# The condition product by samples in two row halves, its second half inside the first group

## Chip, core and metric

One core of one Trainium2 chip runs the kernel. The metric is the device time of one execution, in microseconds (us). The kernel before was timed three times: 1285.14, 1284.44 and 1283.88 us, median 1284.44 us.

## What is computed

```python
W = weights[condition]                     # 32 samples, each picks one of 16 matrices of 64 x 64
c = einsum('bct,bcd->bdt', x, W)           # x: (32, 64, 1024)
h = gelu(einsum('bsd,df->bsf', c, inter_w) + inter_b)   # 1024 -> 4096
out = x + einsum('bsf,fd->bsd', h, output_w) + output_b # 4096 -> 1024
```

All is float32. The 32 samples of 64 rows are 2048 rows of 1024 features for the two large products.

## The kernel before, in words

**The passes.** The rows are worked in two passes `h` of 1024 rows: 8 pairs of samples (`TILES`), two samples of 64 rows to a pair. Each of the two large products is done by a Strassen scheme: 7 products (`PRODUCTS`) in place of 8. Each product takes three matmuls (high by high, high by low, low by high): its operands are split into a float32r part and the rest: ScalarE (ACT) writes the high part with a copy, VectorE (DVE) subtracts it to give the low part. Stage one (`first`, lines 468 to 503) has 8 groups `g` of 512 hidden features with 14 steps `c` each (7 products, two halves `p`); a step is 12 matmuls of 128x512, so a stage of a pass is 1344. Stage two (`second`, lines 505 to 519) has as many.

**The condition product** (`cond`, lines 454 to 466) turns x into the transposed activations y. One matmul takes a pair of samples: a 128x128 block of x is the stationary operand, a row of `wdiag` the moving one, in which the two samples' 64x64 matrices stand on the diagonal. GpSimd (POOL) fills `wdiag` (lines 406 to 420): zeros first, then 32 copies in a loop of 16, each chosen by an index read from `itok_sb`. `cond` runs four times ahead of the first large product: for each pass `h` and each half `n` of its pairs, over 4 pairs and 8 blocks `kb` of features, into all 8 PSUM banks. ACT takes the even banks out, DVE the odd ones (`y_evict`, lines 540 and 696). For pass 0 the four quarters b11, b12, b21, b22 stay in SBUF, and seven operands `y[i]` are made of them (`y_high` 552, `y_low` 708, `y_sum` 713). For pass 1 they go to DRAM by way of `y1_stage` (`y_raw_mem`, SP's lines 299 to 310). During the groups 1 to 6 of pass 0, 28 items (`y1_item`, line 207) of the operands of pass 1 are made on ACT and DVE, five in a group, and stored; for each quarter `kb` of them, seven items, `y1_in` is loaded once (line 278), right behind the store of the seventh item before.

**Weights.** SP loads `w1_raw` for a group in two halves (`load_w1`, line 219); POOL makes three sums `s1_w`, `s2_w`, `s4_w` and one more in place (lines 436 to 449). `high1` (line 561) and `low1` (line 716) split a step's weights into one of three `lhs` buffers, so step `s` can be split when step `s - 3` is done.

**Order.** Each engine's list is written out by hand. An engine runs its list in order; a wait holds all that stands behind it. At the start SP issues, in this order: the indices, one copy of the condition matrices (ACT issues the other), the eight tiles of x of pass 0, the first group's weights, the eight tiles of pass 1, and output_b (lines 291 to 298). PE starts `first` only when all four `cond` are through.

## Time and profile before

| | |
|---|---|
| median of three runs | 1284.44 us |
| profiled execution, its own time | 1285.43 us |
| its span, first to last instruction | 1282.4 us |
| instructions | 15344 |
| PE busy | 1258.2 us (98%) |
| PE weight loads busy | 1043.3 us (81%) |
| DVE busy | 825.2 us (64%) |
| ACT busy | 561.8 us (44%) |
| POOL busy | 194.9 us (15%) |
| mean granted TensorE clock | 0.995 of 2.4 GHz |

PE means TensorE's matmuls and PEld its weight loads. A float32 matmul stands in the trace as two records, each with a load of its own; a float32r matmul as one. Matmuls are pipelined, so the length of a record is more than the distance to the next; a rate is read from a count over a stretch. A row of a timeline merges neighbouring instructions of a kind: start, length from the first start to the last end, line, operands, count, and in brackets the idle time before it and what ended it.

### The profile page before, as it was taken

Reading aid. Unit: us, or ns where it says so; the run is one execution under the profiler, and the core shown is the slowest. Engines: PE = TensorE matmul, PEld = TensorE weight load, DVE = VectorE, ACT = ScalarE, POOL = GpSimd, SP = SyncE. Lnnn points to the kernel's source line nnn. Section 1 sums busy time; section 2 is a strip of 40 time slices with the busy share of each in tenths; the row PEclk is TensorE's granted clock in tenths of the full one; section 3 lists DMA queues with packets and bytes.
Section 4 is the critical chain, followed back from the end, with each engine's and each line's share of the span. In section 5 each row is a group of like instructions: output and inputs, shape, how many; then the busy total and the mean of one; then the engine's idle time right before and its main releaser. Section 6 shows DMA issues by size and latency. Waiting matters only on the chain.

```text
span 1282.4 us, 15344 instructions
## 1 busy us (share of the span) xinstructions
PE 1258.2 (98%) x5634; PEld 1043.3 (81%) x5634; DVE 825.2 (64%) x1078; ACT 561.8 (44%) x949; POOL 194.9 (15%) x105
## 2 busy tenths in 40 slices
PE   7799999999999999999999999999999999999998
PEld 7678888878888888888888888888888888888886
DVE  3857676877477677847665555554547767784764
ACT  3445544544454444444434444444445444444442
POOL 4623331223000000000033333222300000000000
PEclk9899999999999999999999999999999999999999
DMA  9625667654899433228735345443289942233431
GB/s 353 237 89 194 258 236 274 229 200 178 298 393 353 154 99 99 99 99 355 290 141 187 126 180 181 181 153 105 120 296 395 351 155 99 99 99 99 159 125 45
DMA packets 88601, 249.50 MB, mean 195 GB/s; under 512 B 8114, under 2 KB 8146, under 8 KB 87122
## 3 DMA queue, kind: packets, MB, share of 16 engines
q1 hardware_dynamic: 87442, 248.27, 53.3%
q8 instruction: 45, 0.74, 0.2%
q10 hardware_dynamic: 1088, 0.28, 0.1%
q14 instruction: 26, 0.21, 0.1%
HBM read 162.55 MB, written 85.98 MB: 194 GB/s over the span
## 4 chain that ended last, share of the span: by engine, by line
PE 91%; DVE 5%; DMA 3%; issue 1%; ACT 0%; SPq 0%; POOLq 0%; DVEq 0%; POOL 0%
PE ps L516 48%; PE ps L500 42%; DVE lhs L719 1%; PE ps L463 1%; DVE y L711 1%; DMA y_in<-y_raw_mem 1%; DMA h_mem<-c 1%; DMA y_raw_mem<-y_stage 1%; DVE y_whole L714 1%; DVE y_out L821 0%; DMA cond_all<-in_L_cond_weights_dram 0%; DVE y_stage L706 0%; DVE hs L733 0%; DVE y_whole L706 0%; DVE c L726 0%
## 5 line engine op out<-in xcount | busy, mean ns | idle before, releaser
L500 PE MATMUL ps<-y,lhs 128*128 128x512 f32 x2688 | 616.5, 391 | 10.5 <-DVE lhs L719 7.3
L516 PE MATMUL ps<-rhs,lhs 128*128 128x512 f32 x2688 | 609.6, 389 | 0.0
L500 PEld LDWEIGHTS ps<-y,lhs 128*128 128x128 f32 x2688 | 507.1, 189 | 119.5 <-issue 6.4
L516 PEld LDWEIGHTS ps<-rhs,lhs 128*128 128x128 f32 x2688 | 504.5, 188 | 104.8
L640 ACT ACTIVATE lhs<-h_raw 128x512 fp32r<-128x512 f32 x224 | 141.6, 632 | 345.8 <-PE ps L516 340.1
L778 DVE TENSOR_TENSOR lhs<-h_raw,lhs 128x512 fp32r<-128x512 f32 x224 | 155.1, 692 | 188.4 <-ACT lhs L640 188.4
L719 DVE TENSOR_TENSOR lhs<-w_raw,lhs 128x512 fp32r<-128x512 f32 x128 | 106.3, 831 | 132.1 <-ACT lhs L570 132.0
L719 DVE TENSOR_TENSOR lhs<-s_w,lhs 128x512 fp32r<-128x512 f32 x96 | 99.3, 1035 | 89.4 <-ACT lhs L570 89.3
L570 ACT ACTIVATE lhs<-w_raw 128x512 fp32r<-128x512 f32 x128 | 80.7, 632 | 172.1 <-PE ps L500 168.4
L781 DVE TENSOR_TENSOR rhs<-W,rhs 128x512 fp32r<-128x512 f32 x224 | 153.5, 685 | 0.0
L436 POOL TENSOR_TENSOR s_w<-w_raw 128x1024 f32<-128x1024 f32 x16 | 48.7, 3045 | 627.9 <-PE ps L516 354.6
L649 ACT ACTIVATE rhs<-W 128x512 fp32r<-128x512 f32 x224 | 137.9, 616 | 0.0
L570 ACT ACTIVATE lhs<-s_w 128x512 fp32r<-128x512 f32 x96 | 60.6, 631 | 126.6 <-PE ps L500 124.5
L807 DVE TENSOR_TENSOR W<-W,W 128x512 f32<-128x512 f32 x128 | 87.6, 684 | 0.0
L579 ACT ACTIVATE c<-c,b_col 128x512 f32<-128x512 f32 x96 | 68.2, 710 | 6.8 <-DVE c L726 6.7
L726 DVE TENSOR_TENSOR c<-ps,c 128x512 f32<-128x512 f32 x96 | 65.6, 683 | 0.0
L576 ACT ACTIVATE c<-ps 128x512 f32<-128x512 f32 x96 | 55.8, 581 | 7.6 <-DMA h_mem<-c 7.5
L442 POOL TENSOR_TENSOR s_w<-s_w,w_raw 128x1024 f32<-128x1024 f32 x16 | 42.3, 2643 | 39.0 <-DVE lhs L719 38.6
L449 POOL TENSOR_TENSOR w_raw<-w_raw 128x1024 f32<-128x1024 f32 x16 | 46.8, 2922 | 0.0
L448 POOL TENSOR_TENSOR s_w<-w_raw,s_w 128x1024 f32<-128x1024 f32 x16 | 40.9, 2558 | 33.9 <-DVE lhs L719 33.5
L821 DVE TENSOR_TENSOR y_out<-y_in,y_out 128x512 fp32r<-128x512 f32 x28 | 29.7, 1059 | 14.9 <-ACT y_out L659 14.8
L733 DVE TENSOR_TENSOR hs<-c,c 128x1024 f32<-128x1024 f32 x32 | 39.0, 1218 | 0.0
(31 smaller groups left out, 287.7 us busy)
## 6 DMA issues: line engine op xcount, KB each, us to landing
h_raw<-h_mem SPq DMA_DIRECT2D x112, 512.0 KB, 3.4
w_raw<-in_L_ffn_inter_w_dram SPq DMA_DIRECT2D x32, 1024.0 KB, 9.0
h_mem<-hs SPq DMA_DIRECT2D x64, 512.0 KB, 4.9
W<-in_L_ffn_output_w_dram SPq DMA_DIRECT2D x32, 1024.0 KB, 12.7
h_mem<-c SPq DMA_DIRECT2D x48, 512.0 KB, 5.8
y_mem<-y_out SPq DMA_DIRECT2D x28, 512.0 KB, 3.1
y<-y_mem SPq DMA_DIRECT2D x7, 2048.0 KB, 13.6
x<-in_x_dram SPq DMA_DIRECT2D x16, 512.0 KB, 11.4
```

What stands on the lines that cost most here:

```text
L500: last = nc.tensor.matmul(ps[:, bank, :], w[:, k, :], y[i][:, part, k, :], start=(i in FRESH and k == 0 and u == 0), stop=(k == KH - 1 and ...
L516: last = nc.tensor.matmul(ps[:, bank2(h, j, tb), :], lhs[s % RING][:, a, blk(tb)], rhs[r][:, w, :], start=(j in FRESH and q == 0 and u == ...
L570: nc.scalar.activation(split1(s, 0), w1_part(h, g, c), ACT.Copy).then_inc(lhs_hi, 1)
L576: nc.scalar.activation(to[:, p, :], ps[:, bank1(h, g, role, p), :], ACT.Copy).then_inc(copied, 1)
L579: nc.scalar.activation(tile[:, p, :], of, ACT.Gelu_apprx_tanh, bias=b1_col[:, 4 * g + 2 * m + p:4 * g + 2 * m + p + 1]).then_inc(made, 1)
L640: nc.scalar.activation(lhs[s % RING][:, 0, :], of, ACT.Copy).then_inc(lhs_hi, 1)
L649: nc.scalar.activation(rhs[r][:, 0, :], w2_part(j, q), ACT.Copy).then_inc(rhs_hi, 1)
L719: nc.vector.tensor_tensor(split1(s, 1), w1_part(h, g, c), split1(s, 0).bitcast(F32), ALU.subtract).then_inc(lhs_lo, 1)
L726: nc.vector.tensor_tensor(tile[:, p, :], ps[:, bank, :], tile[:, p, :], ALU.add).then_inc(added, 1)
L778: nc.vector.tensor_tensor(lhs[s % RING][:, 1, :], of, lhs[s % RING][:, 0, :].bitcast(F32), ALU.subtract).then_inc(lhs_lo, 1)
L781: nc.vector.tensor_tensor(rhs[r][:, 1, :], w2_part(j, q), rhs[r][:, 0, :].bitcast(F32), ALU.subtract).then_inc(rhs_lo, 1)
L807: nc.vector.tensor_tensor(to[:, pair], a[:, pair], b[:, pair], ALU.subtract).then_inc(t_made[n], 1)
```

## The change

- x of pass 0 comes in two column halves (features 0 to 511, then 512 to 1023), each half followed by half of the first group's weights. Four tiles of x of pass 1 follow; the other four are issued when all of pass 0's condition product is done.
- `wdiag` goes. `w_sel` holds each sample's 64x64 matrix in the 64 partitions that its sample has in x. Sixteen of them (pass 0) are copied by POOL, ACT and DVE in turn (`pick`, `ORDER`), the sixteen of pass 1 come by a DMA each from DRAM, issued by SP with the index in a register.
- A matmul of `cond` takes one sample: 64 rows of x by 128 columns stationary, 64x64 moving. Successive matmuls use the upper and the lower 64 rows in turn and write to two banks; a bank first gets one sample of each pair (`v` = 0), and when all of those are done the other (`v` = 1).
- PE's list begins with the features of the first half of pass 0, then steps 0 and 1 of group 0, then the second half of pass 0 in two calls, then the steps from 2 on; pass 1's condition product is four calls (`cond_two`) behind the steps 3, 5, 7 and 9.
- The first operand is split from PSUM in two halves, and step 0 may begin on the first. The other operands are split and summed in halves too. ACT alone takes out pass 1's results.
- SP loads group 1's weights behind the stores of `y1_stage`; POOL's sums for group 0 don't wait for the condition product.
- `y1_item` has six slots in a group, with two empty ones behind each seventh item.

```diff
-        x1 = at("x1", 128, [TILES, D])
+        x1 = [at(f"x1_{j}", k, [D]) for j, k in enumerate((200, 208, 128, 132, 212, 216, 136, 140))]
...
-        x0 = at("x0", 172, [TILES, D])
-        y1_stage = [at(f"y1_stage{k}", 184 + 8 * k, [KH, BANK]) for k in range(2)]
+        x0 = [at(f"x0_{n}", k, [TB, D]) for n, k in enumerate((128, 184))]
...
+        w_sel = at("w_sel", 156, [PASSES * TILES, C])
         cond_all = at("cond_all", 204, [SETS, C])
-        wdiag = at("wdiag", 208, [PASSES * TILES, P])
...
+        def pick(engine, i):
+            j, s = divmod(i, PER)
+            which = engine.value_load(itok_sb[0:1, i:i + 1], min_val=0, max_val=SETS - 1)
+            rows = slice(s * C, (s + 1) * C)
+            return w_sel[rows, j:j + 1, :], cond_all[rows, bass.ds(which, 1), :]
+        ORDER = [PER * (jj + n * TB) + (n + v) % 2 for v in range(2) for jj in range(TB) for n in range(2)]
...
+        def y1_item(g, c):
+            slot = 6 * (g - 1) + c // 2 - 1
+            kb, i = divmod(slot, PRODUCTS + 2)
+            return kb * PRODUCTS + i if 0 < g < NG - 1 and c in range(2, CHUNKS, 2) and i < PRODUCTS else None
...
-            for j in range(TILES):
-                sp.dma_start(x0[:, j, :], x_tok[0, :, j, :]).then_inc(x0_in[j], 16)
-            load_w1(0, 0)
-            for j in range(TILES):
-                sp.dma_start(x1[:, j, :], x_tok[1, :, j, :]).then_inc(x1_in[j], 16)
+            for k in range(2):
+                cols = slice(k * BANK, (k + 1) * BANK)
+                for j in (0, TB):
+                    sp.dma_start(x0[j // TB][:, :, cols], x_tok[0, :, j:j + TB, cols]).then_inc(x0_in[k], 16)
+                sp.dma_start(w1_raw[0][:, k * KH:(k + 1) * KH, :],
+                             w1_v[:, k * KH:(k + 1) * KH, 0:GROUP]).then_inc(w1_in[0][k], 16)
+            for j in (0, TB, 1, TB + 1):
+                sp.dma_start(x1[j][:], x_tok[1, :, j, :]).then_inc(x1_in[j], 16)
+            sp.wait_ge(itok_in, 16)
+            for i in range(TILES * PER):
+                j, s = divmod(i, PER)
+                which = sp.value_load(itok_sb[0:1, TILES * PER + i:TILES * PER + i + 1], min_val=0, max_val=SETS - 1)
+                sp.dma_start(w_sel[s * C:(s + 1) * C, TILES + j, :],
+                             cond_w[bass.ds(which, 1)].rearrange("o c d -> c (o d)")).then_inc(picked1, 16)
+            sp.wait_ge(cond_done, 2 * KB)
+            for j in (2, TB + 2, 3, TB + 3):
+                sp.dma_start(x1[j][:], x_tok[1, :, j, :]).then_inc(x1_in[j], 16)
+            for k in range(2):
+                sp.wait_ge(kept_act, KB + (k + 1) * KB)
+                for n in range(2):
+                    sp.dma_start(y_raw_mem[:, :, 2 * k + n, :].rearrange("k p t -> p k t"),
+                                 y1_stage[n][:]).then_inc(y1_staged[n], 16)
+            load_w1(0, 1)
             sp.dma_start(b2_all[:], b2.partition_broadcast(P)).then_inc(b2_in, 16)
             for n in range(2):
-                for k in range(2):
-                    sp.wait_ge(y_even, (4 + 2 * n + k + 1) * KH // 2)
-                    sp.wait_ge(y_odd, (4 + 2 * n + k + 1) * KH // 2)
-                    sp.dma_start(y_raw_mem[:, :, 2 * k + n, :].rearrange("k p t -> p k t"),
-                                 y1_stage[k][:]).then_inc(y1_staged[k], 16)
-                if n == 0:
-                    sp.wait_ge(cond_done, 3 * KB)
-                    load_w1(0, 1)
-            for k in range(2):
-                sp.wait_ge(y1_staged[k], 32)
+                sp.wait_ge(y1_staged[n], 32)
             sp.dma_start(y1_in[:], y_raw_mem[0]).then_inc(y1_back, 16)
...
-            nc.gpsimd.memset(wdiag[0:C, :, C:P], 0.0).then_inc(wdiag_zero, 1)
-            nc.gpsimd.memset(wdiag[C:P, :, 0:C], 0.0).then_inc(wdiag_zero, 1)
...
+            for i in ORDER[0::3]:
+                to, of = pick(pool, i)
+                nc.gpsimd.tensor_copy(to, of).then_inc(picked[0], 1)
+            pool.wait_ge(picked[0], len(ORDER[0::3]))
...
-                    else:
-                        pool.wait_ge(cond_done, 2 * KB)
...
+            halves_done = iter(range(2, 99, 2))
+            def cond(h, blocks, bank):
+                for v in range(2):
+                    if v > 0:
+                        pe.wait_ge(cond_half, next(halves_done))
+                    for i in range(len(blocks) * TB):
+                        if h == 0 and blocks[0] == 0:
+                            jj, u = divmod(i, len(blocks))
+                        else:
+                            u, jj = divmod(i, TB)
+                        kb = blocks[u]
+                        if h == 0 and kb == 0:
+                            for e in range(3):
+                                pe.wait_ge(picked[e], len(ORDER[:8 * v + 2 * jj + 2][e::3]))
+                        for n in range(2):
+                            j, s = jj + n * TB, (n + v) % 2
+                            rows = slice(s * C, (s + 1) * C)
+                            of = x0[n][rows, jj, blk(kb)] if h == 0 else x1[j][rows, blk(kb)]
+                            last = nc.tensor.matmul(ps[:, bank[u][n], jj * P + s * C:jj * P + (s + 1) * C], of,
+                                                    w_sel[rows, h * TILES + j, :],
+                                                    start=True, stop=True, skip_group_check=True)
+                            if v == 0 and i == len(blocks) * TB - 1:
+                                last.then_inc(cond_half, 1)
+                            if v == 1 and jj == TB - 1:
+                                last.then_inc(cond_done, 1)
+            def cond_two(h, kb):
+                cond(h, (kb, kb + 1), ((4, 5), (6, 7)))
...
                 elif i == 0 and g == 0:
-                    pe.wait_ge(y_even, 4 * KB // 2)
-                    pe.wait_ge(y_odd, 4 * KB // 2)
+                    pe.wait_ge(kept_dve, 2)
+                elif i == 0:
+                    pe.wait_ge(kept_act, 3 * KB)
+                if i == 1 and h == 0 and g == 0:
+                    pe.wait_ge(kept_dve, KH)
                 if i == 1 and g >= 2:
...
+                    if (h, g, p) == (0, 0, 0) and k % 2 == 0:
+                        pe.wait_ge(y_split, 2 * i + k // 2 + 1)
...
-            pe.wait_ge(wdiag_zero, 2)
             pe.wait_ge(b1_ready, 1)
-            for h in range(PASSES):
-                for n in range(2):
-                    cond(h, n)
+            pe.wait_ge(x0_in[0], 32)
+            cond(0, range(KH), [(4 + kb, kb) for kb in range(KH)])
+            first(0, 0, 0)
+            first(0, 0, 1)
+            pe.wait_ge(x0_in[1], 32)
+            pe.wait_ge(kept_act, KH)
+            pe.wait_ge(y_split, 2)
+            cond_two(0, KH)
+            pe.wait_ge(kept_act, KH + 2)
+            pe.wait_ge(kept_dve, KH + 2)
+            cond_two(0, KH + 2)
+            for c in range(2, CHUNKS):
+                first(0, 0, c)
+                if c % 2 and c < 10:
+                    q = (c - 3) // 2
+                    if q == 0:
+                        for j in range(TILES):
+                            pe.wait_ge(x1_in[j], 16)
+                        pe.wait_ge(picked1, 16 * TILES * PER)
+                        pe.wait_ge(kept_dve, KB)
+                    pe.wait_ge(kept_act, KB + KH * q)
+                    cond_two(1, 2 * q)
             for h in range(PASSES):
                 for g in range(NG):
                     for c in range(CHUNKS):
-                        first(h, g, c)
+                        if (h, g) != (0, 0):
+                            first(h, g, c)
...
+            def y_keep(to, b, bank, done):
+                act.wait_ge(cond_done, done)
+                nc.scalar.activation(to[:, b, :], ps[:, bank, :], ACT.Copy).then_inc(kept_act, 1)
+            def y1_keep(q):
+                for u in range(2):
+                    for n in range(2):
+                        b = 2 * (q % 2) + u
+                        if q == 2 and u == 0:
+                            act.wait_ge(y1_staged[n], 16)
+                        y_keep(y1_stage[n], b, 4 + 2 * u + n, 2 * KB + KH * q + 2 * u + 2)
+            def y_high(i):
+                for u in range(2):
+                    if i == 0:
+                        act.wait_ge(cond_done, 4 * u + 4)
+                        of = ps[:, 4 + 2 * u:6 + 2 * u, :]
...
+                        of = (None, t1_y, t2_y, b22, t3_y, b21, t4_y)[i][:, 2 * u:2 * u + 2, :]
+                    if i in (1, 2, 4, 6):
+                        act.wait_ge(y_t, 2 * (0, 1, 2, 0, 3, 0, 4)[i] + u - 1)
+                    if i == 3:
+                        act.wait_ge(kept_dve, KB)
+                    nc.scalar.activation(y[i][:, 0, 2 * u:2 * u + 2, :], of, ACT.Copy).then_inc(y_hi, 1)
...
-            y_evict(0)
-            y_high(0)
-            y_evict(1)
+            act.wait_ge(itok_in, 16)
+            act.wait_ge(cond_in, 32)
+            for i in ORDER[1::3]:
+                to, of = pick(act, i)
+                nc.scalar.activation(to, of, ACT.Copy).then_inc(picked[1], 1)
             high1(0, 0, 0)
             high1(0, 0, 1)
+            y_high(0)
+            for b in range(KH):
+                act.wait_ge(y_split, b // 2 + 1)
+                y_keep(b11, b, 4 + b, 2 * b + 2)
             y_high(1)
-            y_evict(2)
-            y_high(2)
-            y_evict(3)
+            for b in range(2):
+                y_keep(b21, b, 4 + 2 * b, KB + 2 * b + 2)
+            high1(0, 0, 2)
+            for b in range(2):
+                y_keep(b21, 2 + b, 4 + 2 * b, KB + KH + 2 * b + 2)
+            high1(0, 0, 3)
             for h in range(PASSES):
                 for g in range(NG):
                     for c in range(CHUNKS):
-                        if (h, g) != (0, 0) or c >= 2:
+                        if (h, g) != (0, 0) or c >= 4:
                             high1(h, g, c)
-                        if (h, g) == (0, 0) and 2 <= c < 6:
-                            y_high(c + 1)
+                        if (h, g) == (0, 0) and 4 <= c < 9:
+                            y_high(c - 2)
+                        if (h, g) == (0, 0) and c in (6, 8, 10, 12):
+                            y1_keep(c // 2 - 3)
                         if g > 0:
                             trail(h, g - 1, c)
                         within(h, g, c)
-                        if h == 0 and c in (4, 6, 8, 10, 12) and y1_item(g, c // 2 - 2) is not None:
-                            y1_high(*divmod(y1_item(g, c // 2 - 2), PRODUCTS))
+                        if h == 0 and y1_item(g, c) is not None:
+                            y1_high(*divmod(y1_item(g, c), PRODUCTS))
...
+            def y_keep(to, b, bank, done):
+                dve.wait_ge(cond_done, done)
+                nc.vector.tensor_copy(to[:, b, :], ps[:, bank, :]).then_inc(kept_dve, 1)
+            def y_low(i, u):
+                dve.wait_ge(y_hi, 2 * i + u + 1)
+                half = slice(2 * u, 2 * u + 2)
+                if i == 0:
+                    of = ps[:, 4 + 2 * u:6 + 2 * u, :]
+                else:
+                    of = (None, t1_y, t2_y, b22, t3_y, b21, t4_y)[i][:, half, :]
+                nc.vector.tensor_tensor(y[i][:, 1, half, :], of, y[i][:, 0, half, :].bitcast(F32),
+                                        ALU.subtract).then_inc(y_split, 1)
             def y_sum(to, a, b):
-                nc.vector.tensor_tensor(to[:], a[:], b[:], ALU.subtract).then_inc(y_t, 1)
+                for u in range(2):
+                    half = slice(2 * u, 2 * u + 2)
+                    nc.vector.tensor_tensor(to[:, half], a[:, half], b[:, half], ALU.subtract).then_inc(y_t, 1)
...
+            dve.wait_ge(itok_in, 16)
+            dve.wait_ge(cond_in, 32)
+            for i in ORDER[2::3]:
+                to, of = pick(dve, i)
+                nc.vector.tensor_copy(to, of).then_inc(picked[2], 1)
             low1(0, 0, 0)
             low1(0, 0, 1)
-            y_low(1)
-            y_evict(2)
+            for u in range(2):
+                for b in (2 * u, 2 * u + 1):
+                    y_keep(b12, b, b, 2 * b + 2)
+                y_low(0, u)
+            dve.wait_ge(kept_act, KH)
+            dve.wait_ge(kept_dve, KH)
+            y_sum(t1_y, b12, b11)
+            y_low(1, 0)
+            y_low(1, 1)
+            for b in range(2):
+                y_keep(b22, b, 5 + 2 * b, KB + 2 * b + 2)
+            low1(0, 0, 2)
+            for b in range(2):
+                y_keep(b22, 2 + b, 5 + 2 * b, KB + KH + 2 * b + 2)
+            low1(0, 0, 3)
+            dve.wait_ge(kept_dve, KB)
             y_sum(t2_y, b22, t1_y)
-            y_evict(3)
-            y_low(2)
             for h in range(PASSES):
                 for g in range(NG):
                     for c in range(CHUNKS):
-                        if (h, g) != (0, 0) or c >= 2:
+                        if (h, g) != (0, 0) or c >= 4:
                             low1(h, g, c)
-                        if (h, g) == (0, 0):
-                            if c == 2:
+                        if (h, g) == (0, 0) and 4 <= c < 9:
+                            y_low(c - 2, 0)
+                            y_low(c - 2, 1)
+                            if c == 4:
                                 y_sum(t3_y, b22, b12)
-                                y_low(3)
-                            if c == 3:
-                                y_low(4)
-                            if c == 4:
+                            if c == 6:
+                                dve.wait_ge(kept_act, KB)
                                 y_sum(t4_y, b21, t2_y)
-                                y_low(5)
-                            if c == 5:
-                                y_low(6)
                         if g > 0:
                             trail(h, g - 1, c)
                         if (h, g) == (1, 0) and c == 1:
                             add2(0, 6, 0, 2)
                             add2(0, 6, 1, 2)
                         within(h, g, c)
-                        if h == 0 and c in (3, 5, 7, 9, 11) and y1_item(g, (c - 3) // 2) is not None:
-                            kb, i = divmod(y1_item(g, (c - 3) // 2), PRODUCTS)
+                        if h == 0 and y1_item(g, c + 1) is not None:
+                            kb, i = divmod(y1_item(g, c + 1), PRODUCTS)
                             if i in (1, 2, 4, 6):
                                 y1_sum(kb, {1: 0, 2: 1, 4: 2, 6: 3}[i])
-                        if h == 0 and c in (4, 6, 8, 10, 12) and y1_item(g, c // 2 - 2) is not None:
-                            y1_low(*divmod(y1_item(g, c // 2 - 2), PRODUCTS))
+                        if h == 0 and y1_item(g, c) is not None:
+                            y1_low(*divmod(y1_item(g, c), PRODUCTS))
```

## Rows read from the trace of the kernel before

**Rows 1.** Page, chain that ended last: shares of the span by engine.

```profile
PE 91%; DVE 5%; DMA 3%; issue 1%; ACT 0%; SPq 0%; POOLq 0%; DVEq 0%; POOL 0%
```

**Rows 2.** Timeline of PE: start us, us, engine, line, group, idle before.

```profile
8.13 20.31 PE L463 MATMUL ps<-wdiag,x 128*128 128x128 f32 x160 [2.21 <-POOL wdiag L418]
...
44.08 9.77 PE L500 MATMUL ps<-y,lhs 128*128 128x512 f32 x36 [3.06 <-ACT y_stage L550]
55.04 3.06 PE L500 MATMUL ps<-y,lhs 128*128 128x512 f32 x12 [1.20 <-DVE lhs L719]
...
65.12 3.01 PE L500 MATMUL ps<-y,lhs 128*128 128x512 f32 x12 [0.43 <-DVE lhs L719]
```

**Rows 3.** Timeline of PE behind 70 us.

```profile
70.10 195.43 PE L500 MATMUL ps<-y,lhs 128*128 128x512 f32 x852 [1.97 <-DVE lhs L719]
266.32 2.98 PE L500 MATMUL ps<-y,lhs 128*128 128x512 f32 x12 [0.79 <-DVE lhs L719]
...
362.99 304.80 PE L516 MATMUL ps<-rhs,lhs 128*128 128x512 f32 x1344
```

**Rows 4.** Busy time by stretch of 5 us, with clock, DMA share, GB/s.

```profile
0.00:5.00 5.00, 0.00 (x0) 0.00 (x0) 0.00 (x0) 1.49 (x2) 2.44 (x9) 1.00 0.66 119
5.00:10.00 5.00, 2.50 (x11) 2.40 (x12) 0.19 (x1) 0.00 (x0) 0.93 (x4) 1.00 0.95 358
10.00:15.00 5.00, 5.00 (x35) 5.00 (x35) 0.00 (x0) 0.00 (x0) 1.16 (x5) 1.00 1.03 419
15.00:20.00 5.00, 5.00 (x47) 5.00 (x46) 2.48 (x4) 3.07 (x5) 1.16 (x5) 1.00 1.04 389
20.00:25.00 5.00, 5.00 (x47) 5.00 (x46) 3.79 (x4) 2.57 (x5) 2.61 (x6) 1.00 1.03 401
25.00:30.00 5.00, 4.75 (x43) 4.58 (x43) 4.62 (x5) 2.95 (x4) 3.51 (x5) 1.00 1.03 412
...
70.00:80.00 10.00, 9.90 (x37) 8.06 (x38) 3.95 (x6) 2.37 (x4) 5.10 (x2) 0.83 0.01 2
```

**Rows 5.** Condition product, line 463: durations in ns, min/median/max.

```profile
L463 PE MATMUL ps<-wdiag,x x256: 275/275/553, 8.1 to 40.7; 128*128 128x128 f32 x128
...
L463 PEld LDWEIGHTS ps<-wdiag,x x1: 288/288/288, 8.1 to 8.1; 128*128 128x128 f32 x1
```

**Rows 6.** Bias product, line 523: durations, then both timelines.

```profile
L523 PEld LDWEIGHTS ps<-ident,b_rows x2: 283/308/333, 5.3 to 5.5; 32*128 32x128 f32 x2
L523 PE MATMUL ps<-ident,b_rows x2: 397/407/417, 5.3 to 5.5; 32*128 32x32 f32 x2
...
5.29 0.50 PEld L523 LDWEIGHTS ps<-ident,b_rows 32*128 32x128 f32 x2 [5.29 <-DMA b_rows<-in_L_ffn_inter_b_dram]
...
5.29 0.63 PE L523 MATMUL ps<-ident,b_rows 32*128 32x32 f32 x2 [5.29 <-DMA b_rows<-in_L_ffn_inter_b_dram]
```

**Rows 7.** Evictions, splits and picks by line.

```profile
L706 DVE COPY y_whole<-ps x8: 680/681/692, 16.4 to 25.4; 128x512 f32<-128x512 f32 x8
...
L711 DVE TENSOR_TENSOR y<-y_whole,y x7: 2275/2280/3273, 20.9 to 64.9; 128x2048 fp32r<-128x2048 f32 x7
...
L550 ACT ACTIVATE y_whole<-ps x8: 592/602/618, 16.2 to 24.8; 128x512 f32<-128x512 f32 x8
...
L559 ACT ACTIVATE y<-y_whole x7: 1906/1911/1917, 19.0 to 62.2; 128x2048 fp32r<-128x2048 f32 x7
...
L418 POOL COPY wdiag<-cond_all x32: 229/234/2328, 6.9 to 37.5; - x32
```

**Rows 8.** Timelines of DVE and POOL where both work.

```profile
47.09 2.89 DVE L719 TENSOR_TENSOR lhs<-s_w,lhs 128x512 fp32r<-128x512 f32 x1
...
44.97 4.46 POOL L449 TENSOR_TENSOR w_raw<-w_raw 128x1024 f32<-128x1024 f32 x1
```

**Rows 9.** SP's issues of second-half input.

```profile
13.50 5.08 SPq L297 DMA_DIRECT2D x<-in_x_dram  x7
```

**Rows 10.** Chain of waits near 257 us: start us, us, what.

```profile
257.48 6.71 DMA y_in<-y_raw_mem
```

More of the change, by code:

```diff
@@ L112, in build @@
         b2_in = sem("b2_in")
-        x0_in = [sem(f"x0_in{j}") for j in range(TILES)]
+        x0_in = [sem(f"x0_in{k}") for k in range(2)]
         x1_in = [sem(f"x1_in{j}") for j in range(TILES)]
@@ L118, in build @@
         h_in = [sem(f"h_in{i}") for i in range(HRING)]
-        y1_staged = [sem(f"y1_staged{k}") for k in range(2)]
+        y1_staged = [sem(f"y1_staged{n}") for n in range(2)]
         y1_back = sem("y1_back")
@@ L321, in _ @@
                     if h == 0:
-                        for i in range(5):
-                            if y1_item(g, i) is not None:
-                                keep_y1(y1_item(g, i))
+                        for c in range(CHUNKS):
+                            if y1_item(g, c) is not None:
+                                keep_y1(y1_item(g, c))
                     if g == NG - 1:
```

76 lines of the change are left out of this document (7 added, 69 removed).

## The prediction

> **What bounds the kernel now.** I read the chain of waits by engine first: PE holds 91% of it [rows 1]. Then PE's timeline, to see where it is not held by its own matmuls. One stage of one pass is 1344 matmuls in 304.80 us, 0.2268 us each, and 2.72 us for a step of 12 [rows 3]. Four stages are 1219.2 us; the span is 1282.4, so 63 us lie outside dense work, 5 of them behind the last matmul (it ends near 362.99 + 3 x 304.80 = 1277.4). Nearly all of the rest is in front. The condition product starts at 8.13 and ends about 41 [rows 2, 5]; step 0 starts at 44.08; the steps 0 to 5 (36 + 3 x 12 = 72 matmuls, the third row of 12 is like its neighbours) take till 70.10 in place of 16.3 us, most of it behind DVE, which splits y and weights in one list [rows 2]. From 70.10 to 362.99 there are 1272 matmuls, 288.5 us at the dense rate, and 292.9 passed: 4.4 lost [rows 3]. In 70 to 80 us 37 matmuls started where 44 would fit, 1.9 us lost [rows 4]; 0.3 goes in small steps, and 2.2 around 266 us. There the chain has a reload of `y_in` of 6.71 us between two items that are only 5.4 us (two steps) apart [rows 3, 10]. So group 0 ends at 70.10 + 8 x 2.72 + 1.9 = 93.8. That is the mark for the new order: PE is dense behind it but for the 2.2 us.
>
> **What one record of the condition product costs.** Before, it has 256 records [rows 5], 47 to a stretch of 5 us once warm: 106 ns each [rows 4]. At first nine take from 8.13 to 10 us (11 records in the row, two of them the bias product's), about 210 ns each: the pace of 1.2 GHz, though the column of the granted clock says 1.00. The first 46 end at 15, so about 4 us go at that pace [rows 4]. After the change there are 256 matmuls, 512 records, of 64 columns moving. The stream halves to 53 ns. The weight load need not: each still loads 128 columns of x. The bias product shows a load without a long stream behind it. Its two loads start at 5.29 and 5.29 + 0.50 - 0.333 = 5.46 and end at 5.57 and 5.79 [rows 6]: the second had been under way for 0.12 us when the first ended and ended 0.22 us behind it, with a matmul of only 32 columns between. The first load of the condition product took 288 ns on 128 rows [rows 5], this one 283 ns on 32 [rows 6], so the rows don't matter. I take one load as 0.22 us at 1.2 GHz and 106 ns at 2.4 GHz: as long as the stream was before. Then all hangs on whether the loads of the upper and the lower 64 rows run beside each other. Call p the time of a pair of records, one of each half. Beside each other p is 106 ns, one behind the other 212 ns; and if I misread the load and it is 53 ns, p goes down to 53. No row shows two row halves at work; both ends stay in the range. I take 106.
>
> The Trainium skill speaks on both sides. Its "TensorEngine Tiling (Array Packing)", Key Properties, says different tiles can do weight loads and matmuls in parallel, and its table promises up to 2x for a contraction of 64 or less; by that alone p would be 53, and the time is that of the rival "all halves" below. "TensorE: Matmul & The Clock Gate", What overlaps and what doesn't, says a load overlaps a matmul in flight only where the row group differs. The trace disagrees with that for full rows, where a load and a stream of 106 ns each fit into 106.
>
> **The path of PE, part by part (p = 106).**
> - *First half of x.* The condition matrices (0.54 MB) and half of x (2.10 MB) are 2.64 MB. By 10 us 5 x 119 + 5 x 358 = 2.39 MB had moved, the rest comes at 419 GB/s: 10.6, and 0.7 us to be seen: **11.3** [rows 4]. The same sum gives the first half of the weights at 13.8, x's second half at 19, the other weights at 21.6 and four tiles of pass 1 at 27. Sixteen picks by three engines, at the 0.99 us that POOL needed for one ((37.5 - 6.9) / 31) [rows 7], take 6 us from 5.7: about 11.7, hidden, as PE needs the last ones only in the second part.
> - *Four blocks*, 64 pairs: 4 us at 213 ns, 45 at 106, 0.3 for the wait between the parts (the last matmul's 275 ns [rows 5]): **20.4**. Step 0 and 1's weights are split by 15.
> - *Evictions and the split.* DVE: two evictions at 0.60 (0.68 each, overlapping), a split half at 2.28 / 2 + 0.06 = 1.2, and again, behind ACT's first half of 1.0 [rows 7]: 2.5 and 4.9 us. Step 0 ends at 20.4 + 4.9 + 1.4, plus 0.9 for a fallen clock behind 2.5 us of idleness (the steps 0 to 2 took 9.77 for 8.16 behind 3.06 idle [rows 2]); step 1 at **30.4**.
> - *Second half of pass 0*: two calls of 32 pairs, 3.4 + 0.3 each, and 0.7 for an eviction between: **38.5**. The `y_sum` and `y_low` of operand 1 (4.6 us of DVE) lie beside step 1 and the first call. POOL's sums for group 0, freed of their wait, run from 21.6 to 32; they may slow DVE, as 2.89 us for a 0.68 us subtraction shows beside POOL's 4.46 [rows 8]. Cover: 1 us; without it the cost is up to 2.
> - *Steps 2, 3*: 44.0. *Pass 1's x.* SP issues its last four tiles at 38.5; 2.10 MB at 400 GB/s and 2.3 of latency: 46.1. PE waits 2.1. It is 16 picks later in SP's list: these start near 14 (SP was held back by its ring at first and then needed 0.73 us for a plain issue [rows 9]) and at 1.0 to 1.5 us each, an estimate from a pick's 0.99 and such an issue, end at 30 to 38, just in time. At 2 us each they would cost 7.
> - *Four calls and steps 4 to 13*: 4 x 3.7 + 10 x 2.72 = 42.0: **88.1**. DVE's list from 38.5 (three sums of 2.3, five splits of 2.3, seven weight splits of 0.7) ends at 62.5, always ahead of the steps that need it, since the four calls stretch PE. ACT's 16 evictions of 0.5 sit in front of its copies, 2 us at a time, hidden by two steps.
> - *Group 1's weights*, new on the path. SP waits for ACT's last eviction (77.3 + 1.3), then stores 2.10 MB and loads 2.10 MB. The first half lands at about 89.5, is split by 90.9, and PE wants it at 88.1: 2.8 us. The second half (92.1) goes through POOL's 3 us sum and the split: step 2 waits another 1.2. Together 4, between 1 and 6. Before, these weights were issued at 35.6 and late for nobody.
> - *Items of pass 1*: the two empty slots set a reload and the next item 16.3 us apart, for 6.71 of transfer [rows 10]; the 2.2 us go. The sixth item in a group is 1.7 us of DVE in 38; cover exists, else it costs up to 1.
>
> Sum: 88.1 + 4 - 93.8 = -1.7, and -2.2: **-3.9 us**. In the profiled execution 1285.43 would be 1281.5; that one lies 1.0 above the median of the runs, so against 1284.44 I get **1280.5**. The likeliest case's own range is 1275 to 1286 (DVE's wait, x of pass 1 and group 1's weights each by 2 to 3 us). The sum crosses zero at 3.9 us / 256 pairs = 15 ns: at p = 121.
>
> **Rivals.**
> 1. *Loads one behind the other* (p = 212). Four blocks end at 27.2, the calls take 7.1, the second half of pass 0 ends at 52.1, pass 1's x is there at 59.6, step 13 ends at 59.6 + 28.4 + 27.2 = 115.2, and 119.2 with the weights: 119.2 - 93.8 - 2.2 = +23.2, **1307.6**. For it: no row shows two loads side by side, each matmul's two loads fall on the same half, and the instructions run in order. Against: two halves have rows of their own. It decides from p = 121 on.
> 2. *Partly beside* (p near 160): PE reaches ahead by one load only, so those of one half pair up with half of the others. 256 x 54 ns = 13.8 more than mine: **1294**.
> 3. *All halves* (p = 53, a load of 53 ns or less). Four blocks end at 17.0, pass 0 at 31.7; then SP's picks and x of pass 1 hold PE till 42.5, step 13 ends at 42.5 + 8 + 27.2 = 77.7, 81.7 with the weights: -14.3, **1270**. For it the halved stream; against it [rows 6].
> 4. *The transfers take over at p = 106*: picks at 2 us (+7). Inside the upper part of my range.
>
> **Numbers.** Mine 0.47, rival 1 0.23, rival 2 0.13, rival 3 0.17 (rival 4 is in mine). A change within 0.2% (2.6 us) can't be told from none, so faster means below 1281.9: 0.17 + 0.29 of mine = 0.46. Same (to 1287.0): 0.13 of mine + 0.01 = 0.14. Slower: 0.05 + 0.12 + 0.23 = 0.40. The range 1268 to 1307 leaves out half of rival 1 and little of rival 3.
>
> **What would show it.** The rate of line 463's successor in a call: 64 records in 3.4 us is mine, 6.8 rival 1, 1.7 rival 3. First records near 11.3, step 0 near 23, step 2 near 38.5, its end of group 0 near 88, then an idle PE for 3 us behind `w_raw`, and none around 266. I am wrong if p is far from 106, if PE's first step of group 1 waits for nothing, or if SP's picks end behind 38 us.

## The result: 18 us slower

The kernel after takes 1302.43 us (median of four, 1301.26 to 1303.45) beside 1284.16 of the kernel before: ratio 1.0141, interval 1.0124 to 1.0159. The profiled execution took 1303.45 us, its span is 1300.7. The direction I forecast was wrong. The time lies inside the range and near rival 1's, but by another mechanism than rival 1's.

The timeline of PE of the kernel after answers to [rows 2, 3]. In it line 490 is the condition product, 536 stage one, 552 stage two. By "call" I mean the 64 records of two blocks (`cond_two`).

```profile
11.70 14.25 PE L490 MATMUL ps<-w_sel,x 64*128 64x64 f32 x128 [5.71 <-DMA x<-in_x_dram]
27.59 8.00 PE L536 MATMUL ps<-y,lhs 128*128 128x512 f32 x24 [1.64 <-DVE y L778]
35.52 4.10 PE L490 MATMUL ps<-w_sel,x 64*128 64x64 f32 x64
40.53 5.64 PE L490 MATMUL ps<-w_sel,x 64*128 64x64 f32 x64 [0.91 <-DVE y_whole L769]
46.11 7.36 PE L536 MATMUL ps<-y,lhs 128*128 128x512 f32 x24
55.07 6.23 PE L490 MATMUL ps<-w_sel,x 64*128 64x64 f32 x64 [1.60 <-DMA x<-in_x_dram]
61.23 8.26 PE L536 MATMUL ps<-y,lhs 128*128 128x512 f32 x24
69.42 4.10 PE L490 MATMUL ps<-w_sel,x 64*128 64x64 f32 x64
73.45 5.78 PE L536 MATMUL ps<-y,lhs 128*128 128x512 f32 x24
...
92.92 11.21 PE L536 MATMUL ps<-y,lhs 128*128 128x512 f32 x48
106.68 10.28 PE L536 MATMUL ps<-y,lhs 128*128 128x512 f32 x36 [2.54 <-DVE lhs L789]
120.60 9.66 PE L536 MATMUL ps<-y,lhs 128*128 128x512 f32 x33 [3.64 <-DVE lhs L789]
```

```profile
129.64 251.81 PE L536 MATMUL ps<-y,lhs 128*128 128x512 f32 x1109
381.29 304.80 PE L552 MATMUL ps<-rhs,lhs 128*128 128x512 f32 x1344
```

The reader is to see two things. A call of 64 records takes 4.10 us at 35.52, at 69.42 and in the two calls that follow, but 5.64 and 6.23 us at 40.53 and 55.07, and the first 128 records take 14.25. And group 0 ends at 104.1, after which two idle times of 2.54 and 3.64 us come, with slow rows behind each: 10.28 us for 36 matmuls that take 8.16 at the dense rate. From 104.1 to the end of the stage at 381.3 pass 277.2 us for 266.7 us of dense work. Around 266 us PE no longer waits.

The busy time of line 490 in some stretches shows the clock. The columns are: stretch, its length, PE busy (records), PE's weight loads busy (loads), granted clock, DMA share, GB/s.

```profile
11.80:18.80 7.00, 6.99 (x64) 6.80 (x64) 1.00 1.05 387
42.70:46.10 3.40, 3.40 (x32) 3.29 (x32) 0.51 0.00 0
...
69.40:71.30 1.90, 1.88 (x32) 1.86 (x32) 1.00 0.00 0
```

32 records in 3.40 us is 106 ns each where 0.51 was granted (the level of 1.2 GHz), and 32 in 1.9 is 59 to 62 ns where 1.00 was (2.4 GHz). In the first row 64 records take 7.0 us, 109 ns: the lower level's pace, though the column says 1.00. The same holds at the start in the traces of the kernel before [rows 4] and of `full_rows`, `before_halves`, `same_half` and `n32` below; there the pace has to be read, not the column. The product keeps PE busy for 42.0 us in place of the 32.0 of before; 28.3 of them are the six calls behind step 1.

### The profile page after: what moved, and what is told of

It is laid out like the page before. It is cut to its first block, busy times and chain, and to the rows that moved or that the text cites. A ratio compares the mean times of both kernels' runs of the same rounds, so it can differ in the third digit from the quotient of the medians.

```text
span 1300.7 us, 15802 instructions
## 1 busy us (share of the span) xinstructions
PE 1273.4 (98%) x5890; PEld 1055.2 (81%) x5890; DVE 830.5 (64%) x1086; ACT 568.0 (44%) x969; POOL 173.8 (13%) x76
## 4 chain that ended last, share of the span: by engine, by line
PE 96%; DMA 2%; DVE 1%; SPq 0%; ACT 0%; POOL 0%; issue 0%; DVEq 0%; POOLq 0%; ACTq 0%
PE ps L552 47%; PE ps L536 46%; PE ps L490 3%; DMA x<-in_x_dram 1%; DMA w_raw<-in_L_ffn_inter_w_dram 1%; DVE hs L803 0%; DVE lhs L789 0%; DVE y_out L891 0%; POOL s_w L450 0%; ACT y_stage L597 0%; DVE acc L864 0%; DVE y L778 0%; SPq L322 0%; SPq L238 0%; ACT y L619 0%
## 5 line engine op out<-in xcount | busy, mean ns | idle before, releaser
L789 DVE TENSOR_TENSOR lhs<-w_raw,lhs 128x512 fp32r<-128x512 f32 x128 | 109.8, 859 | 154.2 <-ACT lhs L630 154.1
L789 DVE TENSOR_TENSOR lhs<-s_w,lhs 128x512 fp32r<-128x512 f32 x96 | 92.5, 963 | 90.7 <-ACT lhs L630 90.6
L636 ACT ACTIVATE c<-ps 128x512 f32<-128x512 f32 x96 | 55.8, 581 | 10.5 <-DMA h_mem<-c 10.5
L490 PE MATMUL ps<-w_sel,x 64*128 64x64 f32 x512 | 42.0, 331 | 8.8 <-DMA x<-in_x_dram 7.3
L490 PEld LDWEIGHTS ps<-w_sel,x 64*128 64x128 f32 x512 | 39.9, 242 | 11.9 <-issue 9.2
```

The source lines that it names most:

```text
L490: last = nc.tensor.matmul(ps[:, bank[u][n], jj * P + s * C:jj * P + (s + 1) * C], of, w_sel[rows, h * TILES + j, :], start=True, stop=True ...
L789: nc.vector.tensor_tensor(split1(s, 1), w1_part(h, g, c), split1(s, 0).bitcast(F32), ALU.subtract).then_inc(lhs_lo, 1)
```

## Experiments

**The rows and the order, taken apart.** `full_rows` puts a pair of samples into one matmul again:

```diff
...
-    of = x0[n][rows, jj, blk(kb)] if h == 0 else x1[j][rows, blk(kb)]
-    last = nc.tensor.matmul(ps[:, bank[u][n], jj*P + s*C:...], of, w_sel[rows, ...], ...)
+    of = x0[n][:, jj, blk(kb)] if h == 0 else x1[j][:, blk(kb)]
+    last = nc.tensor.matmul(ps[:, bank[u][n], blk(jj)], of, wdiag[h][:, j, :], ...)
...
```

> The kernel after, with the condition product in full rows again (a pair of samples and a diagonal of matrices to a matmul, as in the kernel before); its order of work, transfers and everything else stay. Theory A: the 64-row matmuls are the loss, for their records run one behind another at 62 ns (124 ns for the work of one full record of 106) and they leave TensorE at its lower clock. Then the first four blocks take about 9 us in place of 14.25, a later call 3.4 in place of 4.10, the clock is up before step 0, and the time falls by 10 to 17 us, to 1286 to 1292. Rival B: the order with its gaps is the loss, and the clock stays low in the same stretches: the first four blocks take 64 records of 213 ns, 13.6 us, and the time stays within 4 us of 1302.

Measured 1295.74 us (ratio to before 1.0086, interval 1.0070 to 1.0101), 6.7 less than after: between what theory and rival say. Its timeline of PE, and two rows of DVE's:

```profile
12.71 9.92 PE L484 MATMUL ps<-wdiag,x 128*128 128x128 f32 x64 [6.63 <-DMA x<-in_x_dram]
...
38.55 5.42 PE L484 MATMUL ps<-wdiag,x 128*128 128x128 f32 x32 [4.17 <-DVE y_whole L761]
...
53.00 6.67 PE L484 MATMUL ps<-wdiag,x 128*128 128x128 f32 x32 [3.53 <-DMA x<-in_x_dram]
...
64.97 3.73 PE L484 MATMUL ps<-wdiag,x 128*128 128x128 f32 x32
...
86.52 11.14 PE L527 MATMUL ps<-y,lhs 128*128 128x512 f32 x48
100.18 10.26 PE L527 MATMUL ps<-y,lhs 128*128 128x512 f32 x36 [2.53 <-DVE lhs L781]
```

```profile
27.53 5.24 DVE L776 TENSOR_TENSOR y_whole<-y_whole,y_whole 128x1024 f32<-128x1024 f32 x2 [1.15 <-ACT y_whole L589]
32.70 4.51 DVE L770 TENSOR_TENSOR y<-y_whole,y 128x1024 fp32r<-128x1024 f32 x2
```

The first 64 full records take 9.92 us, of the same work as 14.25. A later call takes 3.73 us in place of 4.10. But the order has a loss of its own: idle times of 4.17 (DVE), 3.53 (x of pass 1) and 2.53 us (weights of group 1), and behind the first two a call partly or wholly at the lower clock (5.42 and 6.67 us). The 4.17 us are DVE's: two half sums and two half splits, 9.75 us in all beside POOL's sums, stand ahead of the evictions for which PE waits. Group 0 ends at 97.7 us, 6.5 earlier than in the kernel after, and still 9.6 later than I forecast. With the product that before had, this order is 11 us slower than before.

`before_halves` is the other way round, the kernel before with the product in row halves:

```diff
...
+    for v in range(2):                     # all eight blocks, then the other sample of each
+        if v > 0: pe.wait_ge(cond_half, 2 * (r + 1))
         for j in range(n * TB, (n + 1) * TB):
             for kb in range(KB):
+                s = (kb + v) % 2
...
```

> The kernel before with one thing changed: the condition product by samples in row halves, as the kernel after has it, all of it ahead of the first large product. Theory A: 512 records at 62 ns, or at 111 where the clock stays low; the product lasts from 8.1 to between 41 and 65 us, as it started at 8.1 and ended at 41 before, and the time goes up by 5 to 24 us (1289 to 1308), most if the clock doesn't rise in it. Rival B: without the new order's gaps the clock rises after 4 us as before; 512 x 62 = 32 us, which the transfers and evictions before already filled: within 3 us of 1284.

1304.88 us (1.0163, 1.0147 to 1.0178): 20 us dearer. Its busy times by stretch (PE alone, then clock, DMA share, GB/s):

```profile
10.00:30.00 20.00, 19.94 (x182) 1.00 1.03 405
30.00:50.00 20.00, 19.89 (x181) 1.00 0.14 55
...
69.20:73.60 4.40, 4.40 (x11) 1.00 1.03 381
74.00:85.00 11.00, 11.00 (x49) 1.00 0.30 107
```

182 records in 20 us are 110 ns each, and so it goes for 58 us with one gap of 0.57 us. Even the first dense steps behind them run at 400 ns a matmul or a little more (11 in 4.4 us), and only from 74 us on at 224. Here PE was busy nearly all the time and stayed at its lower clock until dense work came. That is the answer to rival B: no gap of the new order is needed for it.

`prewarmed` asks whether row halves let a raised clock fall. It puts four full-row matmuls of 512 columns into the wait for x (`for _i in range(4): nc.tensor.matmul(ps[:, 0, :], flat[:, 0:P], flat[:, 0:BANK], ...)`).

> The kernel after with four full-row float32 matmuls of 512 columns on condition matrices ahead of the first condition product (their result is overwritten), run in the time in which PE waits for x. It asks whether 64-row matmuls let the clock fall or only don't raise it. If they only fail to raise it: the clock is up near 12 us and stays, the 128 records take 8 us in place of 14.25, and the time falls by 6 us or more. If they let it fall: it is up for some of the records only, 10 to 12 us for the 128, and down again before step 0.

```profile
11.70:19.20 7.50, 7.41 (x129) 1.00 1.05 387
21.40:27.00 5.60, 5.60 (x14) 0.52 1.01 378
27.40:29.50 2.10, 2.10 (x10) 1.00 0.12 31
38.60:46.00 7.40, 7.33 (x65) 0.50 0.00 0
```

One run, 1300.58 us, 1.9 under the median of after. With the clock up, the 128 records took 7.67 us, the 8 of my first case. But the clock was down for the dense work right behind (0.52, 14 matmuls in 5.6 us), and the 6.6 us gained by then shrank to 1.9 at the end: steps 0 and 1 took 8.29 us, and PE stood 4.89 us behind DVE. So both: row halves didn't raise the clock, and it fell once they and a gap of 2.05 us were through. Which of the two let it fall, no run shows.

**What a record costs.** In `same_half` successive matmuls keep to one half (`s = v` in place of `s = (n + v) % 2`).

> The kernel after, in which successive matmuls of a part use the same 64 rows (first all lower samples, then all upper) in place of taking turns; the picks are ordered to match. Theory A: nothing of one half runs beside the other anyway, so a part of 32 records takes 1.98 us still and the time stays within 2 us of 1302. Rival C: a load for one half does run beside the stream of the other, and without that a record takes 106 ns or more: a part takes 3.4 us and the time goes up by 10 us or more.

1361.95 us (1.0609, 1.0592 to 1.0625). The 128 first records take 27.86 us, 218 ns each, twice the 111 with turns. So the two halves do run beside each other, and Theory A's serial records are refuted; the 62 ns with turns at the upper clock are half of such a record's time there, some 110, and a little. In `n32` each matmul is cut in two by its moving columns, in `m64` by its stationary ones:

```diff
...
+    for a in range(0, P, 64):              # m64; n32: for a in range(0, C, 32)
+        last = nc.tensor.matmul(ps[a:a + 64, ...], of[:, a:a + 64], w_sel[rows, ...], ...)
...
```

> The kernel after, each matmul of the condition product cut in two by its moving columns (32 of 64): 1024 records, each with a load of 128 columns as before. If the load sets the pace (Theory F), a record keeps its 62 ns (111 at the lower clock) and a call doubles to 8 us. If the stream of 64 columns did (53 ns), a record would fall to about 31 to 40 ns and a call stays near 4.1 to 5 us. Rival G also says 62 ns and 8 us here; the run with 64 stationary columns tells F from G.

> The kernel after, each matmul of the condition product cut in two by its stationary columns (64 of x's 128 to a load): 1024 records. It asks what sets 62 ns a record when two halves take turns at the upper clock. Theory F: the load does (106 to 111 ns for 128 columns in one half, two halves beside each other): half the columns halve it and a record takes about 31 to 40 ns, a call of what were 64 records 4.1 to 5 us. Rival G: a fixed cost for each record does, about 60 ns whatever its size: a call takes twice its 4.10 us, 8 us, and the time goes up by 20 us or more.

`n32`, one run, 1362.04 us: 256 records in 27.83 us, 109 ns each at the lower clock, the same as with twice the stream. `m64`, one run, 1290.85 us, 11.6 less than after. The product's timeline in it, and two stretches:

```profile
12.14 4.97 PE L491 MATMUL ps<-w_sel,x 64*64 64x64 f32 x216 [6.21 <-DMA x<-in_x_dram]
...
39.32 4.08 PE L491 MATMUL ps<-w_sel,x 64*64 64x64 f32 x128 [5.57 <-DVE y_whole L770]
...
61.70 2.44 PE L491 MATMUL ps<-w_sel,x 64*64 64x64 f32 x128
```

```profile
54.20:56.00 1.80, 1.80 (x64) 1.75 (x64) 0.52 0.00 0
...
61.70:62.80 1.10, 1.10 (x64) 1.02 (x64) 1.00 0.00 0
```

128 records in 2.44 us, 18 to 19 ns each. Theory F holds and was too timid: the load sets the pace, and at the lower clock a record of 218 ns alone on its half becomes 111 in turns over two halves and 28 to 32 over four quarters. That is what half the columns in half the time and four quarters beside each other would give, by estimate (218 / 2 / 4 = 27); no run has the two factors apart. The Trainium skill ("TensorEngine Tiling (Array Packing)", Theoretical Speedup) gives up to 2x for one small dimension of 64 or less, and a higher bound where both are small. The runs agree: 2.0 times by halves, 6.8 to 7.8 by quarters with half the columns a record.

**The quarters uncover the next bound.** In `m64` PE waits 5.57 us for DVE before it goes on at 39.32. DVE's timeline there:

```profile
26.39 4.99 DVE L785 TENSOR_TENSOR y_whole<-y_whole,y_whole 128x1024 f32<-128x1024 f32 x2 [1.15 <-ACT y_whole L598]
31.30 6.67 DVE L779 TENSOR_TENSOR y<-y_whole,y 128x1024 fp32r<-128x1024 f32 x2
...
45.24 2.35 DVE L785 TENSOR_TENSOR y_whole<-y_whole,y_whole 128x1024 f32<-128x1024 f32 x2
```

Two half sums took 4.99 us that take 2.35 at 45.24, two half splits 6.67; POOL's sums for group 0 ran from 24.58 to 36.9. In the kernel after, the half splits at 26.23 and 28.56, which read one input from PSUM, took 1.22 us each in the middle of POOL's sums (22.62 to 32.19), and the two half sums behind them, both inputs in SBUF, 3.48. The Trainium skill ("GPSIMD Engine Reference", Specifications) names contention with DVE instructions that have two SBUF inputs; the trace agrees, by the 1.22 and the 3.48 us. `m64_pool_later` lets POOL wait for DVE:

```diff
...
+    else:
+        pool.wait_ge(y_split, 4)
...
```

> The kernel after with quarters (64 stationary columns, 1290.85 us in one run), and POOL's three sums for group 0 held until DVE has split operand 1 (a wait on the fourth half split, which the order of before had in another form). Theory K: beside POOL's sums DVE needed 4.99 us for two half sums that take 2.35 alone and 6.67 for two half splits that take 2.35, 7 us in all, and PE stood 5.57 us behind them; with POOL later both take 2.35, PE's wait shrinks to 1 us or less, and the time falls by 4 to 6 us, to 1285 to 1287. If group 1 then still loses 10 us, the new order with quarters and no such wait is no better than the order of before with the new slots (1281.2). Rival L: POOL comes late for step 2 and the gain is given back: within 1.5 us of 1290.85.

1284.22 us (ratio to before 1.0000, 0.9991 to 1.0009), 6.6 less than the one run of `m64`: Theory K. DVE's two sums took 2.36 us and PE's wait 1.06. The end of group 0, in `m64` and in this run:

```profile
80.21 11.22 PE L537 MATMUL ps<-y,lhs 128*128 128x512 f32 x48
```

```profile
75.20 11.20 PE L539 MATMUL ps<-y,lhs 128*128 128x512 f32 x48
```

So it ends at 91.4 and at 86.4, the latter 7 us ahead of before. All of that was lost again in group 1.

**Group 1.** `w1_first` loads its weights ahead of the second `y1_stage` stores (SP: `if k == 1: wait cond_done, 4 * KB; load_w1(0, 1)`); `full_rows_w1_first` and `q_w1_first` do it with full rows and with quarters.

> The kernel after, with SP's load of group 1's weights issued as soon as pass 1's condition product is done, ahead of the wait for ACT's last evictions and of the second pair of stores of y1_stage (2.1 MB). Theory D: of the 10.5 us that PE loses in the groups 1 and 2 (idle 2.54 and 3.64, and the lower clock behind each), the late weights cause all; they land 6 to 7 us earlier, the first idle time goes, POOL's sums move ahead, and the time falls by 5 to 9 us (1294 to 1297). Rival E: the transfer of y1_in and the first item, now later, hold ACT in turn and give back most: within 2 us of 1302.

> The kernel after with both edits, full rows and the weights first. The two losses are apart in time (before 98 us and behind), so they should add: 1295.7 minus what the weights-first edit alone gains, 1287 to 1291. If it comes under 1284.5, the new order by itself is a gain, which the traces so far don't say.

> The version with quarters and POOL held (1284.2 us), with group 1's weights ahead of the second stores of y1_stage alone. As in the kernel after, the wait moves and nothing is gained: within 2 us of 1284.2.

1302.97, 1296.10 and 1284.96 us: nothing gained in any. The waits of `w1_first` from 104 us on (who waited, for whom: us in total, times, longest):

```profile
ACT c L638 <- DMA h_mem<-c: 8.2, 1, 8.2
ACT y_out L721 <- DMA y_in<-y_raw_mem: 7.4, 1, 7.4
...
PE ps L538 <- ACT c L638: 5.4, 1, 5.4
...
PE ps L538 <- DVE lhs L791: 2.5, 1, 2.5
```

PE no longer waited for the weights at the end of group 0; its steps ran on without a gap to 112.5. The wait moved to ACT's wait for `y_in` and for the store of `c11`, which lies in SP's queue behind group 2's weights. `after_stores_first` and `q_stores_first` put group 0's stores ahead of those weights and output_b behind:

```diff
...
     if g > 0:
         keep_rest(h, g - 1)
+        if (h, g) == (0, 1):
+            load_w1(0, 2)
+            sp.dma_start(b2_all[:], b2.partition_broadcast(P)).then_inc(b2_in, 16)
...
```

> The kernel after with group 1's weights ahead of the second stores of y1_stage (as before: 1303.0 us), and besides SP stores group 0's results before it loads group 2's weights (2.1 MB), and loads output_b behind these. Theory M: the crowd of transfers costs the 10 us in group 1; with the stores ahead ACT's wait of 5.41 us for the store of c11 goes to 1 us or less, and the time falls by 4 to 8 us, 1295 to 1299. Rival N: POOL beside DVE costs it (DVE's 2.5 to 3.4 us for operations of 0.7 to 1.2): PE still waits for a split of DVE in group 1, and the time stays within 2 us of 1302.

> The version with quarters and POOL held, with the weights first, and the stores of group 0 and then output_b as in the first run of this call. By theory M it gains 4 to 8 us on 1284.2: 1276 to 1280, under the order of before with the new slots (1281.2). By rival N it stays at 1283 to 1286.

1307.19 and 1288.51 us, dearer by 4.2 and 3.6 than with the weights first alone. Theory M as I put it failed: ACT's wait for `c11` was 2.5 us, but it waited 7.75 us for `y_in` and 10.88 for the store of an item behind 2.1 MB of weights. `after_items_later` and `q_items_later` also start the items of pass 1 four slots later (`slot = 6 * (g - 1) + c // 2 - 1 - 4`, `divmod(slot, PRODUCTS + 1)`):

> The kernel after with weights first and group 0's stores first (1307.2 us), and the items of pass 1 four slots later, one empty slot behind each seventh in place of two. Theory M (transfers in one queue cost the 10.5 us of group 1): ACT waits for no y_in and no y_mem in group 1; PE's idle times of 2.85 and 7.14 us there go, and the time falls by 10 us or more, to 1291 to 1296, 7 or more under the kernel after. Rival N (POOL beside DVE): an idle time of 3 us behind a DVE split of the weights stays, 1299 to 1303.

> The same two edits on the version with quarters and POOL held (1288.5 us with the stores first). By theory M the time falls to 1274 to 1279, the fastest so far; by rival N it stays at 1282 or above.

1299.27 (1.0113, 1.0097 to 1.0128) and 1281.48 us (0.9981, 0.9971 to 0.9991). Behind group 0 of the first, 3.6 of the 10.5 us came back (stage one ended at 378.1), behind that of the second 5.4 of the 11.0 of `m64_pool_later`. In the first, idle times of 1.54 us (a split of DVE beside POOL: 2.85 us for 0.69) and two near 1.1 (ACT, for the store of `c11`) stayed. Both theories have a share, and I can't give its size: no run took POOL away from DVE in group 1.

**What of it is a gain by itself.** `slots` is the kernel before with the new `y1_item` alone.

> The kernel before with the slots of the pass 1 items alone changed: six in a group, two empty behind each seventh. Theory: the stalls around 266 us go and nothing else moves, 2.2 to 2.5 us faster (1282). Rival: the sixth item in a group makes DVE late elsewhere and gives it back: no change.

1281.18 us, ratio 0.9975 (0.9966 to 0.9985). Its row of PE answers to [rows 3]: no idle time, 1272 matmuls in one piece.

```profile
70.06 288.60 PE L502 MATMUL ps<-y,lhs 128*128 128x512 f32 x1272 [0.41 <-DVE lhs L721]
```

Two attempts to go on from there in the old order:

> The kernel with the new slots in the order of before (1281.2 us), with the 32 picks of wdiag shared: POOL eight, ACT sixteen, DVE eight, all ahead of their evictions. Theory H: POOL's sums for group 0 then run from 24 us in place of 37.8, clear of DVE's splits (one took 2.89 us for 0.68, one 3.27 for 2.28 beside them), and PE waits for no pick: steps 0 to 5 gain 3 us or more, time 1276 to 1279. Rival I: DVE's own list from step 0 on sets those steps in any case, and it begins at the transfer of y1_stage at 42.6 us, which doesn't move: within 1 us of 1281.

> The same, with the condition product in quarters of the array (64 rows by 64 columns, 1024 records, in turn over the four) in the order of before. From the run with 64 stationary columns: 18 ns a record at the upper clock, 30 at the lower, so a round of 256 records takes 4.6 to 8 us in place of 7.1, and PE follows the transfers of x: the product ends near 33 us in place of 41 and step 0 starts 4 to 7 us earlier. Theory: the time falls to 1274 to 1278. Rival I: DVE's list and the transfer of y1_stage set step 0 in any case, and the clock comes up late as with halves: 1281 or more.

1284.72 (0.9997, 0.9985 to 1.0009) and 1293.18 us (1.0066, 1.0053 to 1.0079). In the first POOL's sums moved up beside DVE's sum and splits: two weight splits took 5.60 us and one operand's split 4.42 (for 1.37 and 2.28), and PE stood 7.49 us inside the product behind DVE. In the second they took as long, PE stood 6.43 us behind DVE, 256 records in quarters took 7.65 us at 32.2 (30 ns each, 0.59 granted there), and the product ended at 58.4. There were also three gaps of 2.4 to 3.3 us inside it for which the trace names no releaser. In two of them, and in a gap of 2.82 us at 17.1 in `m64`, the DMA view shows a transfer of the instruction queue (0.02 MB each); whether that is the cause, no run shows. Theory H had the price of the contention right and missed that it moves along. `slots` and `q_items_later` are the fastest, the same within their scatter.

## Why the prediction was wrong

- **The first load of x**: 11.3 forecast, 11.70 measured. Right. The picks were through by 10.5, earlier than forecast, and SP's ended at 36.5, inside 30 to 38 (what had held SP's first issue of x of pass 1 for 4.5 us in the trace before, no row shows). The latencies of ACT and DVE were near: step 0 began 1.64 us behind the blocks, I had 2.5.
- **p, the time of a pair of records**: 106 forecast, 124 (2 x 62) at the upper clock and 222 (against 213) at the lower. The reading of [rows 6] was right: the load counts, and two halves load beside each other. I missed the 18 ns by which a pair is dearer; 256 pairs of them are 4.6 us at most, just over what the forecast had to spare.
- **The failed step is PE's path through group 0**: 88.1 forecast, 104.1 measured. Two terms of it failed.
  - *The clock*, "64 pairs: 4 us at 213 ns, 45 at 106". I carried over the rise after 4 us from a product in full rows (by the 44 records of the product, in place of the 46 with the bias product's two, it is 4.4 us). `before_halves` shows that it doesn't come in 58 us of row halves. The blocks ended at 25.95 in place of 20.4, and steps 0 to 5 and two calls ran wholly or partly at the lower level. What p and the clock cost together in this order is what `full_rows` gives back: 6.5 of the 16 us of group 0.
  - *The waits*, which by themselves turn the forecast gain into a loss (9.6 on -3.9). With full rows and the clock up, group 0 still ended at 97.7, and the time was 1295.7, not 1280.5. The forecast had 0.7 us for an eviction; PE stood 4.17 us behind DVE, whose sums and splits of operand 1 took 9.75 us beside POOL's sums where the forecast had 4.6 and "up to 2" for POOL. It had 7.6 us from the issue of pass 1's last x to its use and 2.1 of waiting; it was 9.0 (44.0 to 53.0) and 3.53. And it had no fallen clock behind either wait: 32 records took 5.42 and 6.67 us in place of 3.73. In the kernel after these waits show as 0.91 and 1.60 us only, as PE comes late to them itself. Quarters, which are cheaper a record too, ended group 0 at 91.4; quarters and POOL held (`m64_pool_later`) ended it at 86.4.
- None of my rivals had the clock, and for the waits my range had 2 to 3 us each. Rival 1's time, 1307.6, came near by accident: its mechanism, loads one behind another, is what `same_half` made, at 1362. That the measured time lies inside my range is luck too, for the upper part of the range was there for rival 1.
- **Group 1's weights**: 4 us forecast (1 to 6), 10.5 measured. I priced the wait for the weights (2.8; it was 2.54) and the first sum, not the other transfers of that moment, nor that DVE would hold a 3.42 us `hs` and a 2.82 us item split beside POOL's sums, nor the fallen clock behind each idle time.
- **Items of pass 1**: 2.2 forecast. `slots` gives 3.0 to 3.3 in the median, and 4.5 in the stage of its trace (358.50 for 362.99; 1.9 of these are the slow start at 70 us [rows 4], which this trace hasn't). Right.
- Sum: +16.0 (group 0) + 6.5 (group 1) on -3.9 is +18.6; measured +18.3 both by medians and by spans.

## What to carry over

A change of the product and a change of the order have to be tried apart: with full rows this order lost 11 us by itself, and row halves in the old order 20. A price for a new kind of matmul needs a clock level beside it: multiply its records by the pace at both levels before believing a gain of a few us. For small products in float32, count the columns of the stationary operand and the parts of the array that load beside each other. A stretch of waits that goes in one place has to be followed through the transfers and the other engines' shared resources until the next dense piece: the quarters' 7 us were lost again in the next group, and two reorderings of transfers only changed which of them was waited for.

## What the runs showed of the hardware

- Nearly uninterrupted work of PE in row halves (64 rows, records of 110 ns) left it at the pace of 1.2 GHz for 58 us (`before_halves`); behind four full-row matmuls of 512 columns (6.3 to 11.7 us) the same records ran at 2.4 GHz (128 in 7.67 us, `prewarmed`).
- A float32 record with a load of 128 columns on one half of the rows: 218 ns at 1.2 GHz (`same_half`); in turns over two halves 111 (62 at 2.4 GHz); with 64 columns in turns over four quarters 28 to 32 (18 to 19, `m64`). The moving columns, 32 or 64, made no difference (109 and 111 ns, `n32`).
- DVE operations with both inputs in SBUF took up to 4 times their time beside POOL's sums (2.85 us for 0.69); those with an input in PSUM did not (1.22 us in the middle of them). POOL's sums grew as well, from 2.4 to 3.3 us in `m64`.
